# Row maximum of attention scores as whole-array products instead of half-height pairs, in a vision transformer block on one core

## What is computed

```python
q = src @ Wq.T + bq
k = src @ Wk.T + bk
v = src @ Wv.T + bv
scores = jnp.einsum('bid,bjd->bij', q, k) * scale
prob = jax.nn.softmax(scores, axis=-1)
out = jnp.einsum('bij,bjd->bid', prob, v)
```

## Time and profile before

| | us |
|---|---|
| runs | 1161.12, 1153.78, 1159.21 |
| median | 1159.21 |
| span of the profiled execution, first to last instruction | 1163.1 |
| TensorE busy | 1029.4 |
| VectorE busy | 902.7 |
| ScalarE busy | 728.6 |
| GpSimd busy | 692.6 |

### The profile page before, as it was taken

The page is one execution under the profiler, slowest core; times in us unless marked ns, Lnnn a source line. Parts: engine busy times, 40 slices in busy tenths (PEclk is TensorE's granted clock), DMA queues, the critical chain, the costliest instruction groups (busy, mean ns, idle before and its releaser), DMA issues.

```text
span 1163.1 us, 18855 instructions
## 1 busy us (share of the span) xinstructions
PE 1029.4 (89%) x5534; PEld 582.2 (50%) x5534; DVE 902.7 (78%) x1847; ACT 728.6 (63%) x1142; POOL 692.6 (60%) x689
## 2 busy tenths in 40 slices
PE   4899999999999999999999999999999999736640
PEld 2455555555555555555555555555555555423320
DVE  5557787789898988889888988898988887654542
ACT  2255455667777777677777776776777667535540
POOL 0014445447676676667767666766666767765665
PEclk8699999999999999999999999999999999866775
DMA  5324335444444443535344443443453613034300
GB/s 129 93 69 106 96 89 141 111 104 111 115 122 115 109 121 96 148 87 150 95 125 120 114 104 106 124 119 101 106 137 79 154 37 92 20 96 121 98 18 10
DMA packets 76732, 118.93 MB, mean 102 GB/s; under 512 B 16652, under 2 KB 52959, under 8 KB 76630
## 3 DMA queue, kind: packets, MB, share of 16 engines
q1 hardware_dynamic: 59798, 100.61, 34.6%
q0 software_dynamic: 16832, 17.11, 4.6%
HBM read 49.64 MB, written 18.11 MB: 58 GB/s over the span
## 4 chain that ended last, share of the span: by engine, by line
PE 55%; DVE 24%; issue 10%; ACT 4%; SPq 2%; another core or an unknown queue 1%; POOL 1%; DMA 1%; POOLq 0%; DVEq 0%; ACTq 0%
PE p_u L575 15%; DVE mx L979 8%; PE p_st L559 8%; PE p_st L562 7%; PE p_sm L545 5%; PE p_misc L508 4%; PE p_misc L531 4%; PE p_misc L638 3%; PE p_misc L654 2%; PE p_misc L590 2%; ACT xh L754 2%; DVE ld L1045 1%; POOL out L1355 1%; DVE tt L1006 1%
## 5 line engine op out<-in xcount | busy, mean ns | idle before, releaser
L1343 POOL DMA_INDIRECT slots<-rows,idx x256 | 261.7, 1022 | 220.5 <-issue 151.4
L771 ACT ACTIVATE pT<-p_st 128x1024 f32<-128x1024 f32 x256 | 262.2, 1024 | 171.9 <-PE p_st L562 131.4
L979 DVE TENSOR_REDUCE mx<-p_sm 128x1 f32<-128x1024 f32 x252 | 307.3, 1220 | 80.1 <-PE p_sm L545 69.5
L1355 POOL DMA_INDIRECT out<-b_o,b_ix x270 | 286.9, 1063 | 111.9 <-issue 73.4
L575 PE MATMUL p_u<-pT,vv 128*64 128x512 f32 x1024 | 263.8, 615 | 0.0
L559 PE MATMUL p_st<-mQ,sK 128*128 128x512 f32 x512 | 184.2, 441 | 5.5 <-ACT pT L771 3.6
L562 PE MATMUL p_st<-mR,sR 72*128 72x512 f32 x512 | 161.8, 397 | 0.0
L545 PE MATMUL p_sm<-sK,mQ 64*128 64x512 f32 x252 | 130.7, 519 | 6.9 <-DVE mx L979 3.4
L559 PEld LDWEIGHTS p_st<-mQ,sK 128*128 128x128 f32 x512 | 79.7, 190 | 104.5 <-issue 81.3
L545 PE MATMUL p_sm<-hi,mQ 64*128 64x512 f32 x252 | 130.6, 518 | 0.0
L562 PEld LDWEIGHTS p_st<-mR,sR 72*128 72x128 f32 x512 | 97.4, 190 | 22.9
(11 more groups left out here) (194 smaller groups left out, 1550.4 us busy)
## 6 DMA issues: line engine op xcount, KB each, us to landing
b_w<-in_w SPq DMA_DIRECT2D x136, 193.5 KB
mQ<-hi SPq DMA_DIRECT2D x64, 256.0 KB
b_in<-slots SPq DMA_DIRECT2D x136, 66.0 KB
sK<-hi SPq DMA_DIRECT2D x32, 256.0 KB
sK<-lo SPq DMA_DIRECT2D x32, 256.0 KB
mR<-lo SPq DMA_DIRECT2D x32, 256.0 KB
sR<-hi SPq DMA_DIRECT2D x32, 256.0 KB
xt<-in_x SPq DMA_DIRECT2D x32, 196.0 KB
```

The costliest lines, as they stand in the source:

```text
L771: act.activation(pT[k % 4][:, :], flat(p_st), ACT.Exp).then_inc(exp_done, 1)
L979: dve.tensor_reduce(mx[:, p, j:j + 1], flat(max_place(n, j)), AX.X, ALU.max).then_inc(max_done, 1)
L1343: pool.indirect_dma_start(slots, bass.IndirectOffsetOnAxis(ap=idx[:, p, j:j + 1], axis=0), rows[:, p, j, :], None, bounds_check=SLOTS - 1, ...
L1355: pool.indirect_dma_start(out_rows, bass.IndirectOffsetOnAxis(ap=b_ix[:, o, j:j + 1], axis=0), b_o[:, o, j, :], None, bounds_check=T - 1, ...
```

## The change

`max_scores` makes both halves with all 128 rows of mQ and of sK. What comes out is high query times the sum of high and low key, so the low key takes part in the maximum. The same banks are written, with as many products and columns, and the order of all instructions stays. `hi` is no longer read by TensorE, and the wait on sm_done before its next write is gone. Lines from 545 on are numbered one lower afterwards, and from 748 on two lower.

```diff
@@ -540,10 +540,9 @@
 
                 after(pe, max_done, j - 1 if isinstance(n, int) and n == 0 else NT * n + j)
 
-                for a, keys in ((0, sK[t]), (1, hi[n % 2])):
-                    h = slice(a * D, (a + 1) * D)
-                    last = pe.matmul(max_place(n, j)[:, a, :], mQ[t][h, j * P:(j + 1) * P],
-                                     keys[h, a * HALF:(a + 1) * HALF], start=True, stop=True)
+                for a in range(2):
+                    last = pe.matmul(max_place(n, j)[:, a, :], mQ[t][:, j * P:(j + 1) * P],
+                                     sK[t][:, a * HALF:(a + 1) * HALF], start=True, stop=True)
                 last.then_inc(sm_done, 1)
 
             def max_turn(n, p):
@@ -745,7 +744,6 @@
                 if not isinstance(n, int) or n >= 2:
                     act.wait_ge(spread_qk[t], 64 * nth + 64)
                     act.wait_ge(spread_r[p], of_parity(n - 2, p, 32))
-                    act.wait_ge(sm_done, NT * n - NT)
                 act.activation(hi[p][:, :], flat(p_misc), ACT.Copy).then_inc(hi_ready, 1)
 
             def split_high(n):
```

## The result

The changed kernel takes 1182.8 us (median of 4 runs, 1180.8 to 1186.6) where the kernel before takes 1160.2 (4 runs, 1153.8 to 1164.7): ratio 1.020, 95% interval 1.016 to 1.023. It is slower by some 23 us; forecast were 20, and the range held it.

What follows compares the result with a forecast made beforehand. TensorE was taken as the bound from image to image. The eight slots, one L545 pair each, sum to +0.80 us a step, over 25 steps +20.0 on 1163.1, so 1183; range 1166 to 1189 (8 in 10).

Steps and rivals of the forecast that it cites:

- The prices of the shapes: Whole-array L545 pair: 0.47 us among its kind, 0.57 or 0.56 with another shape before or behind, 0.66 with both.
- slots 1 and 2: Pair between L590 and L559, forecast -0.11 us a step, and pair between L615 and L575, forecast +0.10.
- Slots 4 and 5: Pair between expert product L638 and L575: L638 must be left and the whole array entered and left, +0.43 us each.
- Slots 1, 3 and 6: Pairs between whole-array products, where changes of shape go away: -0.11 us in the first, -0.15 in each other.
- Slot 7: Pair between half-width L654 and L575, a step's last of eight: +0.22 us, not hidden by waits.
- The full streaming: Rival: every pair costs one more product, 0.23 us, with nothing given back: 57 us, 1216; chance 4%.
- leaving and entering would cost less: Rival: each pair costs just 0.04 us, 10 us or still less in all, 1160 to 1170; chance 13%.
- the loss falls into waits: Rival: savings stay, surcharges behind L638 and L654 fall into TensorE's waits: -7 to -10 us, 1153 to 1156; chance 4%.
- VectorE as the bound: Rival: later reductions make half of the steps grow by another 0.5 us, 6 in all, 1186; chance 14%.
- The wait on sm_done: ScalarE's removed wait, for products issued a step earlier: nothing in either direction.
- Steps 1 to 5: Among the early steps without L638, L654 and L615, where gains and costs nearly cancel: -0.03 us a step.
- the count of changes of shape: Cross-check per step: 24 changes become 18, saving 1.14 us, against 1.86 of lost side-by-side streaming: +0.72.

Runs made afterwards that it cites:

- full_ahead457: Changed kernel with the pair issued right behind the scores, ahead of the expert product, in slots 4, 5 and 7: 1123.2 us, 0.9992 of the kernel before.
- 1124.3: The kernel before, unchanged, recorded again in the later session: 1124.3 us.
- 1138.5: The changed kernel as it is, without the wait on sm_done, in the later session: 1138.5 us, ratio 1.0122 against the kernel before.
- full45: Kernel before with whole-array pairs in slots 4 and 5 only: 1141.6 us, ratio 1.0158.
- full136: Kernel before with whole-array pairs in slots 1, 3 and 6 only: 1118.2 against 1124.1 us, ratio 0.9948.
- before_gaps: Kernel before with VectorE's gate_gaps (L1045) issued ahead of slot 6's maximum instead of behind it: 1122.7 us, ratio 0.9999.
- full027: Kernel before with whole-array pairs in slots 0, 2 and 7 only: 1128.0 us, ratio 1.0042.
- serial64: Kernel before with half-height pairs both on rows 0 to 63, so not side by side: 1173.0 us, ratio 1.043.

## Why the prediction was right, and where not

- **The prices of the shapes.** Right, but for slots 1 and 2: 0.47, 0.57, 0.66 for the pair and 1.06 for L638 stand in the trace to 0.01 to 0.02, and 0.56 where full_ahead457 has it. The 0.66 was a sum that no row showed; the changed kernel's own rows do. Behind the short products of L589 and L614 the pair takes 0.08 to 0.10 more than its price, as if it still had to enter. In slot 1 L589 gives as much back; slot 2 costs 0.16 (L615 and pair from 0.95 to 1.11, medians of the later recordings), not 0.10. The step with no L545 in it was what gave away L638's own cost.
- **Slots 4 and 5 the dearest.** Right, +0.43 forecast. Measured from scores to scores (start of L559 to the next slot's) in the recordings of 1124.3 and 1138.5, median of 12 even steps: 3.42 to 3.85 and 3.44 to 3.87. full45 alone gives 17.6 of its +22, see the cover below.
- **Slots 1, 3 and 6 as gains.** Right in TensorE's own order (L531 0.95 to 0.85, L562 0.56 to 0.47), and full136 is a faster kernel. L590 saved 0.12, not 0.04, but the pair behind it took back 0.08 of it.
- **Slot 7, +0.22, and what hides it.** This is the step that failed. The prediction looked for TensorE's waits in the earlier trace rows, placed them at slots 2 and 3, and held that the 2.3 us that VectorE has to spare in a step cover its later results. One wait was not among those rows: it lies in front of L551, at the end of slot 7 of even steps, and just behind. In the recording of 1124.3, the end of step 16, and TensorE's waits over the whole span:

```profile
529.40 0.27 PE L551 MATMUL p_sm<-c_wide,mx 128*8 128x128 f32 x1 [0.20 <-DVE mx L979]
529.83 0.20 PE L667 MATMUL p_sm<-acc,ones 128*128 128x64 bf16 x1 [0.15 <-DVE ohs L1058]
...
PE p_sm L551 <- DVE mx L979: 3.9, 12, 1.3
...
PE p_sm L667 <- DVE ohs L1058: 1.9, 12, 0.2
```

In the recording of 1138.5 the first of the two waits is left once in place of 12 times, the second not at all. From its scores to L551, slot 7 of the even steps went from 5.57 to 5.51 where +0.22 was forecast, since the kernel before already spent 0.28 there waiting for the last maximum. Two kernels that leave slot 7's products as they are show this wait by itself: it is gone, and slot 7 of even steps takes 5.29, in full45, where TensorE comes 0.86 later, and in before_gaps, where L1045 no longer holds VectorE up. In odd steps, slot 7 does show +0.22 (5.29 to 5.51), but the stretch from L551 to the scores falls from 2.18 to 2.01. Slot 3 of even steps, held by the maximum of slot 2, gained 0.04 instead of 0.15, which works the other way. With that the median step grew by 0.62 (odd) and 0.63 (even), not 0.80, and steps 6 to 30 together by 16.6 us (764.9 to 781.5), not 20.0: net, the overlooked cover is 3.4 us. The same explains the odd sizes of the parts: full027 gives 4 where its prices say 11 to 14 (slot 7 of its even steps stays at 5.57), full45 18 of 22.
- **In the first measurement** steps 6 to 30 grew by 22.0 us, 0.88 a step (778.8 to 800.8), more than those 16.6. There VectorE pauses in odd steps before L1001 (L999 afterwards), and L606 (L605) waits for its tt. The changed kernel, step 15:

```profile
488.51 0.21 DVE L999 RECIPROCAL rs<-p_misc 128x8 f32<-128x8 f32 x1 [1.33 <-remote]
...
490.09 0.63 PE L605 MATMUL p_misc<-c_wide,b_x 128*128 128x128 f32 x4 [1.26 <-DVE tt L1004]
```

The pause is 1.2 to 1.4 us in both (once 2.8) and comes in 8 steps of the kernel before and in 11 of the changed one. The prediction had it in sight: the odd step of the earlier trace rows has 1.3 us in which TensorE is idle, and the sum reckoned with the 0.3 of the even step alone. Had those 1.3 us lain where the cost arises they would have hidden all of it; they lay at L606, in slot 2, and hid none. What VectorE waits for there, the trace does not say ("remote"), and in the later recordings of both neither has it. So the hit of +20 on +23 is partly luck: a cover of 3.4 us that was overlooked, and an amplification of 5.4 that belongs to that measurement. What stays open is the cause of the pause.
- **Rivals.** The full streaming (+57) is out for the whole-array form; only serial64, where side by side alone is taken away, comes near it, +49. That leaving and entering would cost less is out by the rows. That the loss falls into waits is true only at the end of even steps, for slot 7 and the stretch behind L551. VectorE as the bound (+6 more) did not come: TensorE is busy 31.41 of 31.42 us in the changed kernel. It came when TensorE was made faster, in full136.
- **The wait on sm_done**: nothing, as forecast.
- **Steps 1 to 5** fell from 128.33 to 128.02 us, -0.06 a step, forecast -0.03.
- **Small slips in the prediction.** Eight times 0.23 is 1.84, not 1.86, so the count of changes of shape gives +0.70. The times of rivals 1 and 4 start from the median of the runs, that of rival 3 from the profiled span; nothing hangs on either.

## What to carry to other kernels

Whether a product should fill the array is not to be read from the product but from its neighbours: here a whole-array pair instead of a side-by-side half-height one saves about 0.15 us between whole-array products, costs about 0.2 between half-width ones and 0.43 behind a half-height run. Put products of one shape in a row first; that alone made the difference between 1.011 and 0.999 here. And before a cost is booked as lost, list every wait of the bounding engine by place, the ones at the end of a step too, and take an engine's spare time in a step for no cover at a given place: VectorE had 2.3 us to spare and still held TensorE up.

## What was not expected of the hardware

- A VectorE operation of 64 elements with two operands in SBUF takes 0.22 us alone and 1.51 to 1.52 (L1048: 1.82) when it starts just before GpSimd's L1330 (1.06 us), and ends within 0.1 us of the end of L1330 wherever in it it starts; one of 8 elements takes 0.69 instead of 0.17. The Trainium skill (GPSIMD Engine Reference, Specifications) has GpSimd's SBUF interface shared with VectorE, with contention for VectorE instructions in a two-port mode or with two SBUF inputs; the trace agrees, and the reduction of the maximum, whose input is in PSUM, keeps 1.22 throughout.
- The same kernel takes 1160 us in one measurement and 1122 to 1125 in four others, with TensorE's clock at 1.00 in the steps of both recordings. The difference of the two recordings lies in 12 odd steps, 1.0 us each on average (31.52 against 30.55), in two of the even ones, and in 25.6 us of the last stretch. There TensorE is busy 96.4 of 190.0 us against 91.3 of 164.4, at a mean clock of 0.70 against 0.73, so most of it is waiting; for what is open.
- Step 0 varies from execution to execution. Before and after, in the first measurement (columns as in the steps above):

```profile
37.82:65.94 28.12, 26.76 (x95) 13.36 (x96) 13.37 (x11) 11.66 (x14) 0.00 (x0) 0.80 0.26 63
```

```profile
38.69:63.65 24.96, 23.70 (x95) 14.12 (x96) 13.37 (x11) 11.64 (x14) 0.00 (x0) 0.92 0.28 68
```

The granted clock is 0.80 in the one and 0.92 in the other. In the kernel before the clock is at its lower level (0.50) once more from 46 to 52 us; before that TensorE had waited 0.7 us for the exponential in each of two slots, as it did, 0.6 to 0.7 us, in the changed kernel, where it did not fall there. The step takes 26.8 us in the second recording of the kernel before and 25.3 in that of the changed one; other kernels with half-height pairs side by side have 24.8 (full136) to 27.8 us. Whether the change has a part in it is not shown. It makes the difference of the two recorded executions (18.4 us) smaller than that of the medians.
